# Moving a quarter of the product of dx and B from VectorE to GpSimd in a Mamba and mixture-of-experts block

## The chip, the cores and the metric

The kernel runs on one core of one Trainium2 chip. The time is the device time of that core in microseconds, from the first to the last instruction of one execution. Five engines take part: TensorE (PE in the rows), VectorE (DVE), ScalarE (ACT), GpSimd (POOL) and SyncE (SP, which issues the DMAs here). Each engine runs its own instructions in the order of the program and waits on semaphores for the others.

## The reference

The input is x of 8 x 1024 tokens x 256 channels, in float32. Two layers follow, each with a residual:

```python
x = x + layernorm(mamba(layernorm(x)))
x = x + layernorm(moe(layernorm(x)))
```

The part that matters is the state space recurrence in `mamba`, with 512 inner channels d and 16 states s:

```python
dA  = exp(dt[..., None] * A)                    # decay
dBx = dt[..., None] * Bm[:, :, None, :] * xc[..., None]
h   = dA_t * h + dBx_t                          # over 1024 tokens
y_t = einsum('bds,bs->bd', h, C_t)
```

`moe` routes each token to 4 of 16 experts, with a hidden width of 128 in each; all 16 experts are computed for all tokens and weighted.

## The kernel before

The 8192 tokens are cut into 16 chunks of 512 (CH), two per sequence. The program is a software pipeline over phases p from -2 to 17, and each phase has 16 groups, g = 0 to 15. In phase p the recurrence of chunk p runs, one group of (d, s) pairs after another. Beside it stand the projections, the convolution and dt of chunk p + 1, the output projection and the routing of chunk p - 1 and, 26 groups later than the recurrence, one expert per group.

A group G (counted over all phases, 256 in all) holds 128 partitions x 4 blocks x 512 tokens of the state in the tile hs: a partition is a pair of channel and state, and the 4 blocks (beta = 0 to 3, NBETA = 4) are different channels. hs has three buffers (NH). The tile dxr holds dt times xc for four groups (one channel tile M), replicated over the partitions by a DMA, in two buffers; Bb and Cb hold B and C, one slot for each of the four state sets s. A group goes through these steps:

- `inputs(G)`, VectorE, L858: hs = dxr * B for all four blocks at once, one instruction of 128x2048. It adds to the semaphore s_u.
- `decay`, ScalarE, L501: dA = exp(A dt), one block at a time, in two PSUM tiles.
- `scan(G, beta)`, VectorE, L872: h = dA h + hs in place, four instructions of 128x512. dA is read from PSUM. In the second chunk of a sequence it starts from `carry`.
- `read_out(G)`, GpSimd, L761: hs = hs * C, 128x2048. It adds to s_c.
- `add_states(G)`, TensorE, L446: the sum over states into the PSUM tile Y. It adds to s_y, and its buffer of hs is free.

An expert goes from TensorE (`gate` L416, `up` L424) over ScalarE (tanh, L507), VectorE (`expert_gate` L987, `expert_up` L992) and GpSimd (`weigh` L751) back to TensorE (`down` L434).

The order on each engine is written out by hand in loops over the groups. On VectorE, group G is: L987, scan 0, L992, scans 1 to 3, then whatever belongs to this g (L879 gates a finished Y; L831 convolution steps at g = 2 and 3; small statistics at g = 4, 6 and 12; L891 at 5; the routing L924 to L983 at 9; L847, which forms DX, at 10; L1003 at 13), and last `inputs(G + 1)`. GpSimd does per group: wait until s_u shows that `inputs(G)` is done, then `weigh`, then `read_out(G - 1)`. In chunks with an even number (phase without carry) the scans start from zero; in odd ones they read carry.

SP issues the loads of dxr (L227) and Bb (L235); before it overwrites a buffer it waits on s_u for the last product that reads it.

Of the kernel before, what the change touches and what calls it, by code (L numbers as in the profile page):

```python
# [70 lines left out]
def sandwich_kernel(nc, x, w_in, w_out, w_gu, w_dn, w_x, w_rt, cols, alog, ebias, consts, sel_dt, out):  # L71
    with ExitStack() as ctx:
# [7 lines left out]
        def sem(name):  # L80
            return ctx.enter_context(nc.semaphore(name))
# [53 lines left out]
        dxr = sb('dxr', [P, 2, NBETA, CH])  # L135
        Bb = sb('Bb', [P, NSIG, CH])
        Cb = sb('Cb', [P, NSIG, CH])
        hs = sb('hs', [P, NH, NBETA, CH])
# [25 lines left out]
        f_act = Steps(sem('f_act'), ['xT0', 'xT1', 'raw0', 'tap0', 'raw1', 'tap1', 'raw2', 'tap2', 'raw3', 'tap3', 'z0', 'silu_x', 'xd', 'dt', 'z1', 'z2', 'z3', 'silu_z'])  # L164
        f_dve = Steps(sem('f_dve'), [f'c{k}{m}' for m in DVE_CONV for k in range(HIST)] + ['hist', 'dx'])
        fp_full = sem('fp_full')
        s_u, s_dA, s_h, s_keep, s_c, s_y, y_gate = (sem(k) for k in ('s_u', 's_dA', 's_h', 's_keep', 's_c', 's_y', 'y_gate'))
        route = ['den', 'score', 'sfc', 'ps', 't1', 't2', 'gs', 'ggt', 'geq', 'gq', 'ga', 'gr', 'gm', 'tmp', 'top', 'gt', 'eq', 'ng', 'cs', 'cn', 'ok', 'sel', 'w', 'ws', 'we', 'wr', 'comb']
        p_dve = Steps(sem('p_dve'), ['w1', 'nb', 'x1', 'Bw1'] + rsqrt_names('q') + ['Bnb'] + route)
        p_act = Steps(sem('p_act'), ['xn0', 'xn1', 'rev0', 'rev1', 'nm', 'sq', 'ro', 'sum2', 'nm2', 'sq2', 'x2', 'x2T0', 'x2T1', 'sig', 'cmT'])  # L170
# [7 lines left out]
        ld_dx = [sem(f'ld_dx{k}') for k in range(4)]  # L178
        ld_B = [sem(f'ld_B{s}') for s in range(NSIG)]
# [22 lines left out]
        def _(sp):  # L202
# [18 lines left out]
            def load_dx(M, k):  # L221
                if M % MT == 0:
                    sp.wait_ge(st_dx, 16 * (M // MT + 1))
                if M >= 2:
                    sp.wait_ge(s_u, (M - 1) * NSIG)
                src = dx_d.rearrange('(M c k b) t -> M k c (b t)', k=2, b=2, c=CB)[M, k]
                sp.dma_start(dxr[:, M % 2, 2 * k:2 * k + 2, :].rearrange('p b t -> p (b t)'), src.unsqueeze(1).broadcast_to([CB, SG, 2 * CH])).then_inc(ld_dx[2 * (M % 2) + k], 16)  # L227

            def load_B(c, s):
                if s == 0:  # L230
                    sp.wait_ge(st_xd, 16 * (c + 1))
                if c > 0:
# [22 lines left out]
            for p, g, G in groups():  # L255
                c = p + 1
# [488 lines left out]
        @block.gpsimd  # L745
        def _(pool):

            def weigh(q):
                pool.wait_ge(m_w, q + 1)
                pool.wait_ge(ld_cm[q % 2], 16 * (q // 2 + 1))  # L750
                pool.tensor_tensor(th[:, q % NTH, :], th[:, q % NTH, :], cmb[:, q % 2, :], ALU.mult).then_inc(m_a, 1)  # L751

            def read_out(G):
                c, m, s = (G // GPC, G // NSIG % MT, G % NSIG)
                if m == 0:
                    pool.wait_ge(ld_C[s], 16 * (c + 1))
                if c % HALVES < HALVES - 1:
                    pool.wait_ge(s_keep, c // HALVES * GPC + G % GPC + 1)
                else:
                    pool.wait_ge(s_h, (G + 1) * NBETA)  # L760
                pool.tensor_tensor(hs[:, G % NH, :, :], hs[:, G % NH, :, :], Cb[:, s, :].unsqueeze(1).broadcast_to([P, NBETA, CH]), ALU.mult).then_inc(s_c, 1)  # L761
            for p, g, G in groups():
                if 0 <= G < NGRP:
                    pool.wait_ge(s_u, G + 1)
                q = expert_at(G - 2)
                if q is not None:
                    weigh(q)
                if 0 <= G - 1 < NGRP:
                    read_out(G - 1)

        @block.vector
        def _(dve):
# [76 lines left out]
            def inputs(G):  # L849
                c, M, s = (G // GPC, G // NSIG, G % NSIG)  # L850
                if s == 0:
                    for k in range(2):
                        dve.wait_ge(ld_dx[2 * (M % 2) + k], 16 * (M // 2 + 1))
                if M % MT == 0:
                    dve.wait_ge(ld_B[s], 16 * (c + 1))
                if G >= NH:
                    dve.wait_ge(s_y, G - NH + 1)
                dve.tensor_tensor(hs[:, G % NH, :, :], dxr[:, M % 2, :, :], Bb[:, s, :].unsqueeze(1).broadcast_to([P, NBETA, CH]), ALU.mult).then_inc(s_u, 1)  # L858

            def scan(G, beta):  # L860
# [227 lines left out]
```

## Time and profile before

| what | value |
|---|---|
| median of the timed runs | 2791.8 us (3 runs, 2788.87 to 2792.28) |
| span of the profiled execution | 2792.0 us |
| TensorE, VectorE, GpSimd busy | 86%, 88%, 53% |
| L858, product of dx and B | 256 x 2.292 us = 586.6 us on VectorE |
| L761 and L751 | 256 x 4.528 us and 256 x 1.271 us on GpSimd |
| mean granted clock of TensorE | 0.953 |

The profile is of one execution, recorded by the hardware. A row of the timeline gives the start, the duration, the engine, the line of the kernel, what it writes and reads, the shape and the count of instructions merged into it. The idle time before it and what ended that stand in brackets. A window row gives the busy time of each engine in one stretch, with the count of its instructions, then TensorE's granted clock and the DMA share. Busy shares over the whole span mix stretches with different limits, so the rows below are taken from one phase (chunk 8, groups 128 to 143).

### The profile page before, as it was taken

Reading aid. Unit: us, or ns where it says so; the run is one execution under the profiler, and the core shown is the slowest. Engines: PE = TensorE matmul, PEld = TensorE weight load, DVE = VectorE, ACT = ScalarE, POOL = GpSimd, SP = SyncE. Lnnn points to the kernel's source line nnn. Section 1 sums busy time; section 2 is a strip of 40 time slices with the busy share of each in tenths; the row PEclk is TensorE's granted clock in tenths of the full one; section 3 lists DMA queues with packets and bytes.
Section 4 is the critical chain, followed back from the end, with each engine's and each line's share of the span. In section 5 each row is a group of like instructions: output and inputs, shape, how many; then the busy total and the mean of one; then the engine's idle time right before and its main releaser. Section 6 shows DMA issues by size and latency. Waiting matters only on the chain.

```text
span 2792.0 us, 27042 instructions
## 1 busy us (share of the span) xinstructions
PE 2414.2 (86%) x8416; PEld 1179.1 (42%) x8416; DVE 2455.6 (88%) x3265; ACT 1628.2 (58%) x3312; POOL 1474.8 (53%) x516
## 2 busy tenths in 40 slices
PE   4556799898989989899998989899898989988898
PEld 1112254443534444354444435354444445444454
DVE  1799998989899998989989898999989899899642
ACT  3566565666666566665666656665666665654331
POOL 0355564646556564655555465565646556565511
PEclk9677899999999999999999999999999999999999
DMA  1532332425244252524435252433525233352221
GB/s 36 226 107 90 129 139 96 160 94 177 77 144 140 98 170 81 188 74 143 133 105 172 79 184 83 136 130 105 179 79 175 95 124 128 100 177 70 64 76 59
DMA packets 164811, 336.65 MB, mean 121 GB/s; under 512 B 15771, under 2 KB 73404, under 8 KB 156220
## 3 DMA queue, kind: packets, MB, share of 16 engines
q1 hardware_dynamic: 164668, 334.93, 35.8%
q8 instruction: 67, 1.10, 0.2%
q14 instruction: 76, 0.62, 0.1%
HBM read 291.35 MB, written 43.52 MB: 120 GB/s over the span
## 4 chain that ended last, share of the span: by engine, by line
PE 42%; DVE 39%; issue 10%; ACT 9%; DMA 0%; SPq 0%; DVEq 0%; ACTq 0%
DVE hs L872 17%; DVE hs L858 9%; PE Gp L416 8%; PE Up L424 7%; PE MY L434 7%; PE FP L343 5%; PE FP L353 4%; PE FP L379 3%; PE Y L446 3%; DVE th L987 3%; DVE th L992 3%; PE FP L361 1%; ACT XC L571 1%; ACT XB L519 1%; ACT DX L636 1%
## 5 line engine op out<-in xcount | busy, mean ns | idle before, releaser
L761 POOL TENSOR_TENSOR hs<-hs,Cb 128x2048 f32<-128x2048 f32 x256 | 1159.1, 4528 | 203.7 <-DVE hs L858 203.7
L501 ACT ACTIVATE dA<-dtr,A 128x512 f32<-128x512 f32 x1024 | 699.7, 689 | 771.3 <-DVE hs L872 768.7
L751 POOL TENSOR_TENSOR th<-th,cmb 128x512 f32<-128x512 f32 x256 | 325.4, 1271 | 1096.8 <-DVE hs L858 980.7
L872 DVE TENSOR_TENSOR_SCAN hs<-dA,carry,hs 128x512 f32<-128x512 f32 x512 | 627.2, 1264 | 31.7 <-ACT dA L501 31.4
L416 PE MATMUL Gp<-x2T,Wgu 128*128 128x512 f32 x1024 | 530.4, 642 | 129.2 <-DVE th L987 129.0
L872 DVE TENSOR_TENSOR_SCAN hs<-dA,hs 128x512 f32<-128x512 f32 x512 | 596.2, 1203 | 50.6 <-ACT dA L501 50.1
L858 DVE TENSOR_TENSOR hs<-dxr,Bb 128x2048 f32<-128x2048 f32 x256 | 586.6, 2292 | 13.4 <-DMA dxr<-dx_d 12.3
L434 PE MATMUL MY<-Wdn,th 128*128 128x256 f32 x2048 | 486.3, 380 | 0.0
L424 PE MATMUL Up<-x2T,Wgu 128*128 128x512 f32 x1024 | 486.2, 597 | 0.0
L434 PEld LDWEIGHTS MY<-Wdn,th 128*128 128x128 f32 x2048 | 383.6, 190 | 136.5 <-issue 84.6
L416 PEld LDWEIGHTS Gp<-x2T,Wgu 128*128 128x128 f32 x1024 | 183.6, 198 | 473.4 <-issue 259.1
L446 PE MATMUL Y<-hs,Cst 128*32 128x512 f32 x2048 | 291.0, 642 | 21.5 <-POOL hs L761 21.5
L343 PE MATMUL FP<-xT,Win 128*128 128x512 f32 x512 | 262.1, 636 | 49.6 <-ACT SZ L565 15.8
L424 PEld LDWEIGHTS Up<-x2T,Wgu 128*128 128x128 f32 x1024 | 190.7, 192 | 260.8 <-issue 208.4
L987 DVE SCALAR_TENSOR_TENSOR th<-th,Gp 128x512 f32<-128x512 f32 x256 | 173.5, 678 | 68.1 <-ACT th L507 68.1
L507 ACT ACTIVATE th<-Gp 128x512 f32<-128x512 f32 x256 | 149.0, 582 | 114.8 <-PE Gp L416 114.8
L992 DVE TENSOR_TENSOR th<-Up,th 128x512 f32<-128x512 f32 x256 | 170.0, 664 | 10.0 <-PE Up L424 9.3
L343 PEld LDWEIGHTS FP<-xT,Win 128*128 128x128 f32 x512 | 95.8, 199 | 193.9 <-issue 94.5
L353 PE MATMUL FP<-XB,Kdiag 128*128 128x512 f32 x256 | 121.6, 620 | 11.6 <-ACT XB L551 11.6
L379 PE MATMUL FP<-Wout,SZ 128*128 128x256 f32 x512 | 122.6, 383 | 3.1 <-ACT DX L611 3.1
L379 PEld LDWEIGHTS FP<-Wout,SZ 128*128 128x128 f32 x512 | 98.0, 192 | 31.2 <-issue 14.3
L446 PEld LDWEIGHTS Y<-hs,Cst 128*32 128x32 f32 x2048 | 41.2, 110 | 149.5 <-issue 109.0
(131 smaller groups left out, 1827.1 us busy)
## 6 DMA issues: line engine op xcount, KB each, us to landing
dtr<-dt_d SPq DMA_DIRECT2D x64, 1024.0 KB, 5.5
dxr<-dx_d SPq DMA_DIRECT2D x128, 512.0 KB, 7.2
cmb<-cm_d SPq DMA_DIRECT2D x256, 256.0 KB, 3.6
Wdn<-in_w_dn SPq DMA_DIRECT2D x256, 128.0 KB, 3.5
dt_d<-XB SPq DMA_DIRECT2D x16, 1024.0 KB, 4.3
dx_d<-DX SPq DMA_DIRECT2D x16, 1024.0 KB, 5.8
Bb<-bc_d SPq DMA_DIRECT2D x64, 256.0 KB, 3.1
Cb<-bc_d SPq DMA_DIRECT2D x64, 256.0 KB, 4.0
```

What stands on the lines that cost most here:

```text
L343: mm = pe.matmul(FP[:, :], Win[:, q, c0:c0 + P], xT[:, q, :], start=q == 0, stop=q == KM - 1)
L379: pe.matmul(o, SZ[:, c % 2, m, b * P:(b + 1) * P], Wout[:, m, :], start=m == 0, stop=False)
L416: mm = pe.matmul(Gp[:, :], Wgu[:, k, e, 0:DE], x2T[:, c % 2, k, :], start=k == 0, stop=k == KM - 1)
L424: mm = pe.matmul(Up[:, :], Wgu[:, k, e, DE:2 * DE], x2T[:, c % 2, k, :], start=k == 0, stop=k == KM - 1)
L434: mm = pe.matmul(MY[b // 2][:, (b % 2) * DM:(b % 2 + 1) * DM], th[:, q % NTH, b * P:(b + 1) * P], Wdn[:, q % NWD, :], start=e == 0 and b % ...
L446: mm = pe.matmul(Y[beta * CB:(beta + 1) * CB, :], sel_y, hs[:, G % NH, beta, :], start=False, stop=s == NSIG - 1, tile_position=(0, beta * ...
L501: act.activation(dA[h % 2][:, :], dtr[:, M % 2, beta, :], ACT.Exp, scale=A[:, k:k + 1]).then_inc(s_dA, 1)
L751: pool.tensor_tensor(th[:, q % NTH, :], th[:, q % NTH, :], cmb[:, q % 2, :], ALU.mult).then_inc(m_a, 1)
L761: pool.tensor_tensor(hs[:, G % NH, :, :], hs[:, G % NH, :, :], Cb[:, s, :].unsqueeze(1).broadcast_to([P, NBETA, CH]), ALU.mult).then_inc(s ...
L858: dve.tensor_tensor(hs[:, G % NH, :, :], dxr[:, M % 2, :, :], Bb[:, s, :].unsqueeze(1).broadcast_to([P, NBETA, CH]), ALU.mult).then_inc(s_ ...
L872: dve.tensor_tensor_scan(hv, dA[h % 2][:, :], hv, first, ALU.mult, ALU.add).then_inc(s_h, 1)
L987: dve.scalar_tensor_tensor(out=th[:, q % NTH, :], in0=th[:, q % NTH, :], scalar=1.0, in1=Gp[:, :], op0=ALU.add, op1=ALU.mult).then_inc(m_v, 1)
```

## The change

The product of dx and B is split. VectorE forms it for the blocks 0 to 2 of a group (128x1536), and GpSimd forms it for block 3 (128x512) in the new `last_input(G + 1)`, at the end of its group G, behind `read_out(G - 1)`. It waits for the same loads and the same free buffer (s_y) as VectorE's part, and adds to a new semaphore s_u3. The scan of block 3 waits for s_u3, and so do SP's loads into dxr and Bb. GpSimd's wait at the top of its group is on s_u alone, as before.

```diff
@@ SP: load_dx, load_B
                     sp.wait_ge(s_u, (M - 1) * NSIG)
+                    sp.wait_ge(s_u3, (M - 1) * NSIG)
...
                     sp.wait_ge(s_u, c * GPC - NSIG + s + 1)
+                    sp.wait_ge(s_u3, c * GPC - NSIG + s + 1)
@@ GpSimd
+            def last_input(G):
+                c, M, s = (G // GPC, G // NSIG, G % NSIG)
+                if s == 0:
+                    pool.wait_ge(ld_dx[2 * (M % 2) + 1], 16 * (M // 2 + 1))
+                if M % MT == 0:
+                    pool.wait_ge(ld_B[s], 16 * (c + 1))
+                if G >= NH:
+                    pool.wait_ge(s_y, G - NH + 1)
+                pool.tensor_tensor(hs[:, G % NH, NBETA - 1, :], dxr[:, M % 2, NBETA - 1, :], Bb[:, s, :], ALU.mult).then_inc(s_u3, 1)
...
                 if 0 <= G - 1 < NGRP:
                     read_out(G - 1)
+                if 0 <= G + 1 < NGRP:
+                    last_input(G + 1)
@@ VectorE: inputs, scan
-                dve.tensor_tensor(hs[:, G % NH, :, :], dxr[:, M % 2, :, :], Bb[:, s, :].unsqueeze(1).broadcast_to([P, NBETA, CH]), ALU.mult).then_inc(s_u, 1)
+                dve.tensor_tensor(hs[:, G % NH, 0:NBETA - 1, :], dxr[:, M % 2, 0:NBETA - 1, :], Bb[:, s, :].unsqueeze(1).broadcast_to([P, NBETA - 1, CH]), ALU.mult).then_inc(s_u, 1)
...
+                if beta == NBETA - 1:
+                    dve.wait_ge(s_u3, G + 1)
                 dve.wait_ge(s_dA, h + 1)
```

GpSimd's order before, in a phase with experts; th is the expert's activation, hs the state:

```order
L761 TENSOR_TENSOR hs<-hs,Cb 128x2048 [waits s_h,ld_C0]
L751 TENSOR_TENSOR th<-th,cmb 128x512 [waits ld_cm0,m_w,s_u]
L761 TENSOR_TENSOR hs<-hs,Cb 128x2048 [waits s_h,ld_C1]
L751 TENSOR_TENSOR th<-th,cmb 128x512 [waits ld_cm1,m_w,s_u]
L761 TENSOR_TENSOR hs<-hs,Cb 128x2048 [waits s_h,ld_C2]
```

GpSimd's order now; L753 is the old L751, L773 the old L761, L763 the new product:

```order
L753 TENSOR_TENSOR th<-th,cmb 128x512 [waits ld_cm1,m_w,s_u]
L773 TENSOR_TENSOR hs<-hs,Cb 128x2048 [waits s_h]
L763 TENSOR_TENSOR hs<-dxr,Bb 128x512 [waits s_y]
L753 TENSOR_TENSOR th<-th,cmb 128x512 [waits ld_cm0,m_w,s_u]
L773 TENSOR_TENSOR hs<-hs,Cb 128x2048 [waits s_h]
L763 TENSOR_TENSOR hs<-dxr,Bb 128x512 [waits s_y]
```

The product stands behind the read-out of the group before and ahead of the wait on s_u that opens the next group.

VectorE's order before, at the end of group 9 and in group 10 of a phase with carry:

```order
L983 SCALAR_TENSOR_TENSOR comb<-DX 128x64 [waits p_dve,fp_full]
L879 TENSOR_TENSOR SZ<-Y,SZ 128x512 [waits s_y]
L858 TENSOR_TENSOR hs<-dxr,Bb 128x2048 [waits s_y]
L987 SCALAR_TENSOR_TENSOR th<-th,Gp 128x512 [waits m_th]
L872 SCALAR_TENSOR_TENSOR hs<-dA,carry,hs 128x512 [waits s_dA,s_keep,s_u]
L992 TENSOR_TENSOR th<-Up,th 128x512 [waits m_v,m_u]
L872 SCALAR_TENSOR_TENSOR hs<-dA,carry,hs 128x512 [waits s_dA] x3
L847 TENSOR_TENSOR DX<-XB,XC 128x2048 [waits p_dve,f_act]
```

The same place now; L872 is the shortened product, L888 the scan, L1003 and L1008 the old L987 and L992, L861 the old L847:

```order
L999 SCALAR_TENSOR_TENSOR comb<-DX 128x64 [waits p_dve,fp_full]
L895 TENSOR_TENSOR SZ<-Y,SZ 128x512 [waits s_y]
L872 TENSOR_TENSOR hs<-dxr,Bb 128x1536 [waits s_y]
L1003 SCALAR_TENSOR_TENSOR th<-th,Gp 128x512 [waits m_th]
L888 SCALAR_TENSOR_TENSOR hs<-dA,carry,hs 128x512 [waits s_dA,s_keep,s_u]
L1008 TENSOR_TENSOR th<-Up,th 128x512 [waits m_v,m_u]
L888 SCALAR_TENSOR_TENSOR hs<-dA,carry,hs 128x512 [waits s_dA] x2
L888 SCALAR_TENSOR_TENSOR hs<-dA,carry,hs 128x512 [waits s_dA,s_u3]
L861 TENSOR_TENSOR DX<-XB,XC 128x2048 [waits p_dve,f_act]
```

Nothing changes its place on VectorE; the product is shorter, and the last scan has a wait more.

## Rows read from the trace of the kernel before

**Rows 1.** The page: span, then busy us (share of the span) and instructions of each engine.
```profile
span 2792.0 us, 27042 instructions
...
PE 2414.2 (86%) x8416; PEld 1179.1 (42%) x8416; DVE 2455.6 (88%) x3265; ACT 1628.2 (58%) x3312; POOL 1474.8 (53%) x516
```

**Rows 2.** The page, costliest groups: count | busy us, mean ns | idle before, releaser.
```profile
L761 POOL TENSOR_TENSOR hs<-hs,Cb 128x2048 f32<-128x2048 f32 x256 | 1159.1, 4528 | 203.7 <-DVE hs L858 203.7
...
L751 POOL TENSOR_TENSOR th<-th,cmb 128x512 f32<-128x512 f32 x256 | 325.4, 1271 | 1096.8 <-DVE hs L858 980.7
...
L858 DVE TENSOR_TENSOR hs<-dxr,Bb 128x2048 f32<-128x2048 f32 x256 | 586.6, 2292 | 13.4 <-DMA dxr<-dx_d 12.3
```

**Rows 3.** Windows, cut at ends of L858: groups 0, 1-6, 7-8, 9, 10 to 14; last phase.
```profile
core 0: us, PE busy (x) PEld busy (x) DVE busy (x) ACT busy (x) POOL busy (x), PEclk, DMA share, GB/s
1336.65:1344.63 7.98, 6.29 (x24) 3.69 (x24) 7.98 (x9) 4.34 (x9) 5.75 (x2) 1.00 0.99 344
1344.63:1407.05 62.42, 62.42 (x219) 32.40 (x217) 58.80 (x83) 39.59 (x104) 34.56 (x12) 1.00 0.26 83
1407.05:1427.66 20.61, 17.05 (x61) 7.81 (x60) 15.98 (x17) 14.62 (x22) 11.54 (x4) 0.92 0.41 141
1427.66:1443.37 15.71, 15.50 (x66) 7.50 (x63) 14.55 (x40) 9.32 (x14) 5.74 (x2) 1.00 0.14 41
1443.37:1453.55 10.18, 8.49 (x32) 4.06 (x32) 10.18 (x9) 3.85 (x7) 5.76 (x2) 1.00 0.24 88
1453.55:1461.53 7.98, 7.27 (x23) 3.49 (x20) 7.98 (x8) 4.35 (x8) 5.75 (x2) 1.00 0.64 232
1461.53:1472.72 11.19, 9.53 (x39) 4.09 (x37) 10.01 (x21) 9.41 (x28) 5.77 (x2) 1.00 0.20 59
1472.72:1482.30 9.58, 7.55 (x26) 3.33 (x26) 9.58 (x10) 5.93 (x8) 5.75 (x2) 1.00 0.79 281
1482.30:1490.27 7.97, 6.42 (x24) 3.03 (x24) 7.97 (x8) 6.26 (x11) 5.75 (x2) 1.00 0.64 190
...
2487.91:2496.00 8.09, 7.45 (x26) 4.95 (x27) 8.09 (x8) 3.28 (x5) 5.76 (x2) 1.00 0.14 49
```

**Rows 4.** Timeline, a bare period without carry: start us, us, engine, line [idle before].
```profile
1482.38 1.27 POOL L751 TENSOR_TENSOR th<-th,cmb 128x512 f32<-128x512 f32 x1 [3.84 <-DVE hs L858]
...
1483.60 4.52 POOL L761 TENSOR_TENSOR hs<-hs,Cb 128x2048 f32<-128x2048 f32 x1
...
1484.53 3.44 DVE L872 TENSOR_TENSOR_SCAN hs<-dA,hs 128x512 f32<-128x512 f32 x3
...
1487.89 2.38 DVE L858 TENSOR_TENSOR hs<-dxr,Bb 128x2048 f32<-128x2048 f32 x1
```

**Rows 5.** Timeline, a bare period with carry.
```profile
1329.86 4.52 POOL L761 TENSOR_TENSOR hs<-hs,Cb 128x2048 f32<-128x2048 f32 x1
...
1334.39 2.26 DVE L858 TENSOR_TENSOR hs<-dxr,Bb 128x2048 f32<-128x2048 f32 x1
```

**Rows 6.** Timeline, after the last scans: GpSimd at work as L891 is issued.
```profile
2657.18 1.26 POOL L751 TENSOR_TENSOR th<-th,cmb 128x512 f32<-128x512 f32 x1 [9.59 <-DVE th L992]
...
2657.85 1.68 DVE L891 TENSOR_TENSOR x<-DX,x 128x1024 f32<-128x1024 f32 x1 [0.75 <-ACT DX L629]
```

**Rows 7.** Timeline, VectorE, group 13: L1003, GpSimd idle.
```profile
1478.88 1.21 DVE L1003 TENSOR_TENSOR x<-my,x 128x1024 f32<-128x1024 f32 x1
```

**Rows 8.** Timeline, group 9.
```profile
1433.36 1.07 PE L446 MATMUL Y<-hs,Cst 128*32 128x512 f32 x8
...
1434.55 0.23 DVE L928 TENSOR_TENSOR DX<-DX,Ebias 128x64 f32<-128x64 f32 x1
```

**Rows 9.** Timeline, VectorE, group 12.
```profile
1467.96 0.17 DVE L801 TENSOR_SCALAR z_w<-z_s 128x4 f32<-128x4 f32 x1 [0.77 <-ACT XB L519]
```

**Rows 10.** Timeline, group 3: VectorE frees Gp, TensorE fills it again.
```profile
1363.16 0.68 DVE L987 SCALAR_TENSOR_TENSOR th<-th,Gp 128x512 f32<-128x512 f32 x1
...
1367.31 1.98 PE L416 MATMUL Gp<-x2T,Wgu 128*128 128x512 f32 x4
```

More of the change, by code:

```diff
@@ L166, in sandwich_kernel @@
         fp_full = sem('fp_full')
-        s_u, s_dA, s_h, s_keep, s_c, s_y, y_gate = (sem(k) for k in ('s_u', 's_dA', 's_h', 's_keep', 's_c', 's_y', 'y_gate'))
+        s_u, s_u3, s_dA, s_h, s_keep, s_c, s_y, y_gate = (sem(k) for k in ('s_u', 's_u3', 's_dA', 's_h', 's_keep', 's_c', 's_y', 'y_gate'))
         route = ['den', 'score', 'sfc', 'ps', 't1', 't2', 'gs', 'ggt', 'geq', 'gq', 'ga', 'gr', 'gm', 'tmp', 'top', 'gt', 'eq', 'ng', 'cs', 'cn', 'ok', 'sel', 'w', 'ws', 'we', 'wr', 'comb']
```

## The prediction, made before the changed kernel ran

> **What bounds the kernel now.** I read the page's busy times first [rows 1]: TensorE 86% and VectorE 88% of a span of 2792.0 us, GpSimd 53%. No engine is full over the whole span, so the question is which is full where. The costliest groups come next [rows 2]: the product of dx and B on VectorE takes 2.292 us 256 times, and GpSimd has two jobs per group, 4.528 us (h times C) and 1.271 us (weighting an expert). Then I cut one phase (16 groups) into periods, each from the end of one L858 to the end of the next [rows 3]. Four kinds of stretch appear:
> - Groups 1 to 6, 62.42 us: TensorE is busy all of it. VectorE has 3.6 us of idle time.
> - Groups 7 and 8, 20.61 us: a chain over ScalarE and TensorE up to the routing sigmoid. VectorE idles 4.6 us.
> - Groups 9 to 15, 1427.66 to 1498.25: VectorE is busy 68.3 of 70.6 us (group 15 reads like 14; 10, 11, 13, 14 and 15 have no gap). It sets the end there.
> - Group 0: VectorE is full, and TensorE's long stretch starts from its last scan.
> So only time on VectorE in groups 9 to 15 counts directly: 7 periods per phase. I call a period bare when VectorE does only L987, four scans, L992 and L858: 7.97 us without carry (even phases), 8.1 us with it (odd phases; the last window of rows 3 is one).
>
> **The sizes.** A product of 128x2048 takes 2.26 us undisturbed [rows 5], a two-input one of 128x1024 takes 1.21 us [rows 7]; the line between them gives 1.21 + (2.26 - 1.21)/2 = 1.74 us for 128x1536. VectorE saves 0.53 us per group (0.48 to 0.57 if the fixed part is off). The same shape on GpSimd, all operands in SBUF, is L751: 1.27 us [rows 2]. Its work per period becomes 1.27 + 4.53 + 1.27 = 7.05 us. The new wait of scan 3 on s_u3 costs nothing: the product is ready at the latest 1.3 us into the next period, and scan 3 starts some 4.3 us into it [rows 4].
>
> **What GpSimd and VectorE do to each other.** This decides the sign. VectorE's L891 is issued 0.67 us into GpSimd's L751 and takes 1.68 us [rows 6]; its twin in shape takes 1.21 us alone [rows 7]. The overlap is 2657.18 + 1.26 - 2657.85 = 0.59 us, the extra is 0.47 us: L891 did nothing until 0.12 us before GpSimd's end. Sharing at half speed would have given only 0.30 us. The product L858 shows it too: in rows 4 it starts 0.23 us before L761's end and takes 2.38 instead of 2.26 us, 0.12 us more. Scans, L987 and L992, which take one input from PSUM, run inside L761 at their usual time (3.44 us for three) [rows 4]. So a VectorE operation with two SBUF inputs waits for a GpSimd operation in progress. Today the wait on s_u at the top of GpSimd's loop starts its two jobs just after L858, and L761 ends 5.82 us into the period (1483.60 + 4.52 - 1482.30), while L858 is ready at 5.59 us without carry (1487.89 - 1482.30) and at 5.84 with it (L761 begins 1.30 us into a period, so that of rows 5 began at 1328.56, and L858 starts at 1334.39): they just miss each other. The new product takes exactly the place behind L761, 5.78 to 7.05 us, where L858 stands.
>
> No row shows the opposite case, GpSimd arriving while VectorE holds. The Trainium skill (SBUF — State Buffer, "SBUF: two separate sides") says that whichever of the two starts first has the shared pair for its whole instruction and the other is fully blocked; by that the sum is the one below, 2831 us, and without the blocking of GpSimd it is that of rival B.
>
> **Sum, even phase** (times within the period; the change against today):
> - Bare, GpSimd on time: L858 has waited since 5.59, goes at 5.70, ends 7.44: -0.53. The product follows at 7.4 and reaches 1.25 us into the next period.
> - Bare, GpSimd 1.25 late: L761 ends at 6.95, L858 runs 6.83 to 8.57, the product after it again: +0.59.
> - Group 9: a routing chain of 27 small operations follows the sigmoid, which it already waits for, so what groups 7 and 8 save is absorbed. GpSimd's product needs s_y, raised by TensorE's L446, which ends 1434.43; then it runs for 1.27 us just as L928 (two SBUF inputs) is due at 1434.55 [rows 8]. L928 waits about 1.05 us: +1.05 - 0.53 = +0.52.
> - Group 10: L847 (2.3 us, two SBUF inputs) takes the place at 5.70 to 7.96, the waiting product 7.9 to 9.2, L858 9.1 to 10.83 against 10.18: +0.65.
> - Group 11, bare: -0.53.
> - Group 12: L801, due at 6.43 [rows 9], is held to 6.83, the product enters between two small operations and holds the chain until 8.05; 2.26 us of it are left, then 1.74: 12.05 against 11.19: +0.86.
> - Group 13: L1003, due at 6.16 [rows 7], waits to 6.93: +0.77 - 0.53 = +0.24.
> - Groups 14 and 15, bare: -0.53 and +0.59.
> Sum +1.80 us.
>
> **Odd phase**: the scans are longer, L858 is due at 5.84, after the product has started; every bare period waits to 6.93 and ends at 8.67: +0.57, with no backlog. Group 9 +0.52, group 10 +0.56, 11 +0.57, 12 -0.16, 13 -0.02, 14 and 15 +0.57 each. Sum +2.61 us.
>
> Mean 2.2 us, times 14 phase changes, is 31 us. The last phase has no next front to feed and 8 bare periods of 8.1 us, of which the last of [rows 3] is one: 8 x 0.57 = 5 us. The first phases run without L751 and partly wait for a slow start; I take 3 us (0 to 8). Total +39 us on 2792.0 us: 2831 us. The median of the timed runs, 2791.8 us, lies 0.2 us from the profiled span, so nothing is added.
>
> **What stays hidden.** In groups 0 to 3 VectorE falls behind by 0.6 + 0.1 + 1.7 + 0.7 = 3.1 us, because the three L831 of groups 2 and 3 (two SBUF inputs) meet the product too. TensorE has 1367.31 - 1363.84 = 3.5 us between L987 and the gate matmul that waits for it [rows 10], and VectorE catches up in its idle time of groups 4 and 6. I cost this at nothing; without the cover it is 1 to 3 us per phase. SP's loads of dxr and B now wait for s_u3 as well, up to 1.25 us later; they are issued two or more periods ahead: nothing.
>
> **Rivals.**
> A. The cover of groups 1 to 6 fails (TensorE waits for L987 or for ScalarE's evacuations behind late scans): +1 to +3 us in 14 phases, 2845 to 2870 us. For it: 3.1 of 3.5 us of slack are used. Against: the delays come stepwise, and VectorE idles in 4.
> B. GpSimd is never held by VectorE: it keeps its schedule, no backlog. Even bare periods all give -0.53, group 10 -0.53, group 12 -0.04: the even sum is -1.4, the odd stays; mean +0.6, 14 x 0.6 + 5 + 3 = 16: 2808 us. Nothing in the trace excludes it.
> C. The other side: the two do not hinder each other, or the product mostly falls into gaps. Then VectorE's 0.53 us counts in groups 9 to 15 in full: 14 x 7 x 0.53 = 52, and some 15 periods at both ends 8: 2732 us. GpSimd's 7.05 us would fit under 7.44. It decides from the point where the wait on GpSimd is under 0.53 us per period; rows 4 and 6 speak against it.
> D. Small operations pay nothing (only whole L858, L847 and L1003 are held): group 9 -0.53, group 12 -0.15; sums -0.3 and +1.6, mean +0.65, total 2809 us, or with luck in 0 to 3 no change at all.
> E. The change does not do what it says, for instance because scan 3 waits for s_u3 and the time moves there: same as A in size.
>
> **How the numbers follow.** Forecast 0.60 with its own range 2818 to 2845; A (with E) 0.16; B and D together 0.15, of which a third ends within 0.2% (5.6 us, what a measurement can tell from no change); C and smaller gains 0.09. The range of 2802 to 2868 us takes in B, D and most of A. Slower 0.60 + 0.16 + 0.10 = 0.86, same 0.05, faster 0.09.
>
> **What would show it.** L858's successor with 1.74 us alone, but a mean well above that (about 2.3 to 2.7 us with the waits), its overlap with GpSimd ending 0.12 us before GpSimd does. Bare periods of 7.44 and 8.57 in turn in even phases, 8.67 in odd ones. GpSimd's busy share from 53% to about 65%. Group 9 longer by 0.5 us, with one small operation of about 1.2 us. Groups 1 to 6 unchanged at 62.4 us. It is wrong if L858's successor starts and ends at 1.74 us while GpSimd's product is running, or if bare periods fall below 7.6 us in odd phases.

## The result: 0.8% slower, 22 us of the 39 forecast

| | before | after |
|---|---|---|
| median of 4 runs each, us | 2792.04 (2788.87 to 2794.82) | 2813.85 (2812.87 to 2814.76) |
| ratio, 95% interval | | 1.0079 (1.0065 to 1.0093) |
| span of the profiled execution, us | 2792.0 | 2811.9 |

The forecast was 2831 us with a range of 2802 to 2868. The direction holds, and so does the mutual blocking of the two engines; the size was forecast 1.8 times too large. Half of the miss lies in the phases with carry (odd), where a step of the forecast failed. The time lies in the range all the same.

In the changed kernel the lines of the program have moved: L753 is the old L751 (weighting an expert), L763 GpSimd's new product, L773 the old L761 (h times C), L872 VectorE's product (old L858), L888 the scans (old L872), L944 and L946 the old L928 and L930 of the routing. First its page: the busy times and four of the costliest groups, in the columns of [rows 1] and [rows 2].

```profile
span 2811.9 us, 27803 instructions
...
PE 2421.8 (86%) x8416; PEld 1181.7 (42%) x8416; DVE 2493.3 (89%) x3265; ACT 1627.8 (58%) x3312; POOL 1986.5 (71%) x772
...
L773 POOL TENSOR_TENSOR hs<-hs,Cb 128x2048 f32<-128x2048 f32 x256 | 1158.2, 4524 | 60.0 <-DVE hs L872 60.0
...
L763 POOL TENSOR_TENSOR hs<-dxr,Bb 128x512 f32<-128x512 f32 x256 | 527.5, 2060 | 100.8 <-DMA dxr<-dx_d 83.5
L872 DVE TENSOR_TENSOR hs<-dxr,Bb 128x1536 f32<-128x1536 f32 x256 | 506.5, 1978 | 12.2 <-DMA dxr<-dx_d 12.1
...
L845 DVE SCALAR_TENSOR_TENSOR XC<-XB,Cols,XC 128x512 f32<-128x512 f32 x96 | 112.5, 1172 | 14.3 <-ACT XC L557 12.0
```

VectorE has a quarter less of the product to form and yet is busy 38 us longer than in [rows 1]. That is what blocking looks like here: not as idle time but as long instructions. The product means 1.978 us where 1.76 is its undisturbed mean (an experiment below), L763 2.060 us where the same shape takes 1.27 in L753, and L845, which nobody touched, went from 753 ns (L831) to 1172.

Next the windows of the changed kernel, cut as [rows 3]: two bare periods of an odd phase, then an even phase with its groups 0, 1 to 6, 7 and 8, 9, 10, 11, 12, 13, 14 and 15.

```profile
core 0: us, PE busy (x) PEld busy (x) DVE busy (x) ACT busy (x) POOL busy (x), PEclk, DMA share, GB/s
1325.21:1332.77 7.56, 6.48 (x24) 3.03 (x24) 7.56 (x8) 5.55 (x9) 7.49 (x3) 1.00 0.54 193
1332.77:1341.22 8.45, 6.55 (x24) 3.03 (x24) 8.45 (x8) 4.83 (x9) 8.45 (x4) 1.00 0.53 176
1341.22:1349.67 8.45, 6.78 (x28) 3.85 (x32) 8.45 (x8) 4.83 (x9) 8.45 (x4) 1.00 0.93 326
1349.67:1412.84 63.17, 62.72 (x220) 32.74 (x213) 60.77 (x83) 39.59 (x104) 45.41 (x19) 1.00 0.26 83
1412.84:1431.62 18.78, 15.22 (x55) 7.01 (x54) 14.89 (x16) 14.12 (x22) 14.37 (x6) 0.91 0.46 154
1431.62:1448.81 17.19, 16.07 (x68) 7.83 (x66) 14.99 (x40) 9.24 (x14) 8.18 (x4) 1.00 0.15 48
1448.81:1459.53 10.72, 9.32 (x40) 4.06 (x32) 10.72 (x9) 3.85 (x7) 9.03 (x3) 1.00 0.23 80
1459.53:1466.97 7.44, 6.41 (x17) 3.00 (x18) 7.44 (x8) 4.29 (x8) 7.36 (x3) 1.00 0.70 233
1466.97:1478.91 11.94, 10.07 (x41) 4.58 (x39) 10.77 (x21) 9.02 (x29) 8.08 (x4) 1.00 0.20 56
1478.91:1488.72 9.81, 8.98 (x26) 4.08 (x26) 9.81 (x10) 6.59 (x9) 6.97 (x3) 0.83 0.79 281
1488.72:1496.17 7.45, 6.42 (x24) 3.04 (x24) 7.45 (x8) 5.53 (x10) 7.38 (x3) 1.00 0.63 194
1496.17:1504.61 8.44, 6.49 (x24) 3.03 (x24) 8.44 (x8) 4.90 (x10) 8.44 (x4) 1.00 0.58 177
```

The first bare period behind a gap of GpSimd takes 7.44 to 7.56 us and each further one 8.44 or 8.45, group 0's among them; in those GpSimd has no idle time at all (8.45 of 8.45). The even phase from group 0 to 15 is 163.39 us; the same windows before add up to 161.59 [rows 3, with group 15 as long as 14]: +1.80. In groups 1 to 9 the cuts shift against one another because L872 isn't on the path there; take only their sum. GpSimd's 71% on the page is not work alone: by its undisturbed means it has 7.07 us of work per group, the rest is waiting inside its rows.

The timeline of the changed kernel shows how a short and a long period arise (start us, us, engine, line). Even phase, GpSimd:

```profile
1490.02 4.53 POOL L773 TENSOR_TENSOR hs<-hs,Cb 128x2048 f32<-128x2048 f32 x1
1494.51 2.78 POOL L763 TENSOR_TENSOR hs<-dxr,Bb 128x512 f32<-128x512 f32 x1
1497.25 1.26 POOL L753 TENSOR_TENSOR th<-th,cmb 128x512 f32<-128x512 f32 x1
1498.48 4.52 POOL L773 TENSOR_TENSOR hs<-hs,Cb 128x2048 f32<-128x2048 f32 x1
```

and VectorE's products of the two periods:

```profile
1494.31 1.85 DVE L872 TENSOR_TENSOR hs<-dxr,Bb 128x1536 f32<-128x1536 f32 x1
...
1501.76 2.85 DVE L872 TENSOR_TENSOR hs<-dxr,Bb 128x1536 f32<-128x1536 f32 x1
```

L872 is issued 0.24 us before L773 ends (1490.02 + 4.53 = 1494.55), waits 0.1 us and runs to 1496.16. GpSimd's product, listed from 1494.51, takes 2.78 us instead of 1.27: it stood still until L872 was through and ends 1.13 us after it. So L753 starts 1.08 us into the period, where L751 started at 0.08 [rows 4], L773 ends at 1503.00, and the next L872, ready at 1501.76, takes 2.85 us. From there it repeats: in the run of bare periods at the start of the last phase of the recurrence GpSimd's read-out comes every 8.45 us. In the same columns:

```profile
2488.85 4.52 POOL L773 TENSOR_TENSOR hs<-hs,Cb 128x2048 f32<-128x2048 f32 x1
2493.32 2.79 POOL L763 TENSOR_TENSOR hs<-dxr,Bb 128x512 f32<-128x512 f32 x1
...
2497.31 4.52 POOL L773 TENSOR_TENSOR hs<-hs,Cb 128x2048 f32<-128x2048 f32 x1
...
2505.76 4.51 POOL L773 TENSOR_TENSOR hs<-hs,Cb 128x2048 f32<-128x2048 f32 x1
```

Start to start: 1.23 us from L753 to L773, 4.47 to L763, 2.76 with the wait to the next L753. That is a loop in which L753, L773, L872 and L763 follow one another and none beside another, 8.45 us in all, where VectorE alone would need 7.44 (5.70 and 1.74). GpSimd *is* held by VectorE. The Trainium skill (SBUF — State Buffer, "SBUF: two separate sides") says so: whichever starts first holds the pair of SBUF ports that the two share for its whole instruction. By that rule, the trace agrees: 2.78 us against 1.27.

Group 9 in the changed kernel, one row of TensorE, one of GpSimd, two of VectorE:

```profile
1438.40 1.07 PE L448 MATMUL Y<-hs,Cst 128*32 128x512 f32 x8
...
1439.58 1.35 POOL L763 TENSOR_TENSOR hs<-dxr,Bb 128x512 f32<-128x512 f32 x1 [1.13 <-PE Y L448]
...
1439.58 0.23 DVE L944 TENSOR_TENSOR DX<-DX,Ebias 128x64 f32<-128x64 f32 x1
1439.84 1.14 DVE L946 TENSOR_TENSOR DX<-DX 128x32 f32<-128x32 f32 x1
```

The wait that was forecast is there, on the next small operation: L946 takes 1.14 us; the next operation of its shape, L947, takes 0.18, and before it was 0.19 for L930.

The rest I read phase by phase, by two stretches: front, from the last scan of group 0 to the end of the routing sigmoid, and back, from there to the last scan of the next group 0. Ends of rows, us:

| | front even | front odd | back even | back odd |
|---|---|---|---|---|
| before | 91.37 | 91.15 | 70.47 | 71.32 |
| after | 91.85 | 91.98 | 71.80 | 71.72 |
| change | +0.48 | +0.83 | +1.33 | +0.40 |

These are phases 4 to 8. Of those behind them all but one read otherwise in the changed kernel: front 90.2 or 93.2 us, back up to 72.7, which over two phases adds up to within 0.7 us of the same (see the last section). The mean of the two kinds is (1.81 + 1.23) / 2 = 1.52 us. The whole difference of the spans, 19.8 us, I cut at the last scan of group 0 of a phase. Up to that of phase 1 the changed kernel is 3.2 us ahead (219.00 against 222.20). The 14 phase changes from there to phase 15 give +18.6 (14 x 1.52 would be 21; phase 1 alone gives -0.7), and what is behind gives +4.4: 2.0 in the groups of phase 15 and 2.4 after its last scan.

### The profile page after: what moved, and what is told of

It is laid out like the page before. It is cut to its first block, busy times and chain, and to the rows that moved or that the text cites. A ratio compares the mean times of both kernels' runs of the same rounds, so it can differ in the third digit from the quotient of the medians.

```text
span 2811.9 us, 27803 instructions
## 1 busy us (share of the span) xinstructions
PE 2421.8 (86%) x8416; PEld 1181.7 (42%) x8416; DVE 2493.3 (89%) x3265; ACT 1627.8 (58%) x3312; POOL 1986.5 (71%) x772
## 4 chain that ended last, share of the span: by engine, by line
PE 40%; DVE 39%; issue 11%; ACT 9%; POOL 0%; DMA 0%; DVEq 0%; SPq 0%; ACTq 0%; POOLq 0%
DVE hs L888 16%; DVE hs L872 8%; PE Gp L418 7%; PE MY L436 6%; PE Up L426 6%; PE FP L345 6%; PE FP L355 4%; PE FP L381 3%; DVE th L1008 3%; DVE th L1003 3%; PE Y L448 3%; PE FP L363 1%; ACT XC L573 1%; ACT XB L521 1%; ACT dA L503 1%
## 5 line engine op out<-in xcount | busy, mean ns | idle before, releaser
L773 POOL TENSOR_TENSOR hs<-hs,Cb 128x2048 f32<-128x2048 f32 x256 | 1158.2, 4524 | 60.0 <-DVE hs L872 60.0
L753 POOL TENSOR_TENSOR th<-th,cmb 128x512 f32<-128x512 f32 x256 | 324.7, 1269 | 647.8 <-DVE hs L872 530.3
L888 DVE TENSOR_TENSOR_SCAN hs<-dA,carry,hs 128x512 f32<-128x512 f32 x512 | 626.6, 1262 | 28.4 <-ACT dA L503 28.0
L418 PE MATMUL Gp<-x2T,Wgu 128*128 128x512 f32 x1024 | 542.8, 655 | 111.8 <-DVE th L1003 111.8
L888 DVE TENSOR_TENSOR_SCAN hs<-dA,hs 128x512 f32<-128x512 f32 x512 | 595.7, 1202 | 43.5 <-ACT dA L503 42.8
L763 POOL TENSOR_TENSOR hs<-dxr,Bb 128x512 f32<-128x512 f32 x256 | 527.5, 2060 | 100.8 <-DMA dxr<-dx_d 83.5
L872 DVE TENSOR_TENSOR hs<-dxr,Bb 128x1536 f32<-128x1536 f32 x256 | 506.5, 1978 | 12.2 <-DMA dxr<-dx_d 12.1
L1003 DVE SCALAR_TENSOR_TENSOR th<-th,Gp 128x512 f32<-128x512 f32 x256 | 173.3, 677 | 71.2 <-ACT th L509 71.2
L1008 DVE TENSOR_TENSOR th<-Up,th 128x512 f32<-128x512 f32 x256 | 169.8, 663 | 9.3 <-PE Up L426 8.7
L845 DVE SCALAR_TENSOR_TENSOR XC<-XB,Cols,XC 128x512 f32<-128x512 f32 x96 | 112.5, 1172 | 14.3 <-ACT XC L557 12.0
```

The costliest lines, as they stand in the source:

```text
L418: mm = pe.matmul(Gp[:, :], Wgu[:, k, e, 0:DE], x2T[:, c % 2, k, :], start=k == 0, stop=k == KM - 1)
L763: pool.tensor_tensor(hs[:, G % NH, NBETA - 1, :], dxr[:, M % 2, NBETA - 1, :], Bb[:, s, :], ALU.mult).then_inc(s_u3, 1)
L872: dve.tensor_tensor(hs[:, G % NH, 0:NBETA - 1, :], dxr[:, M % 2, 0:NBETA - 1, :], Bb[:, s, :].unsqueeze(1).broadcast_to([P, NBETA - 1, CH] ...
L1003: dve.scalar_tensor_tensor(out=th[:, q % NTH, :], in0=th[:, q % NTH, :], scalar=1.0, in1=Gp[:, :], op0=ALU.add, op1=ALU.mult).then_inc(m_v, 1)
```

## The experiments

Ratios are against the kernel before on the same chip. Where a short condition stands for an edit, the waits on s_u3 are counted to match.

**1. VectorE's saving alone.**
```
-                if 0 <= G + 1 < NGRP:
-                    last_input(G + 1)
+            dve.memset(hs[:, :, NBETA - 1, :], 0.0)     # once, at the start
...
-                if beta == NBETA - 1:
-                    dve.wait_ge(s_u3, G + 1)
```


> The saving alone: VectorE forms the product for the blocks 0 to 2, and nobody forms it for block 3 (its state stays zero, so its part of y is missing from the result). No GpSimd operation and no s_u3 is added. Theory L (the two engines exclude each other, and VectorE's time counts in groups 9 to 15 and in the product at the end of group 0): 8 x 0.53 us per phase and some 20 periods at both ends, 2792 - 14 x 4.2 - 10 = about 2723 us; bare periods 7.44 us (even) and 7.56 us (odd). Rival W (the saving on VectorE is worth little, because ScalarE or TensorE is next in those groups): 2760 to 2790 us.


Measured 2730.1 us, 0.9782 (0.9767 to 0.9796). Its page:
```profile
span 2729.4 us, 27043 instructions
...
L869 DVE TENSOR_TENSOR hs<-dxr,Bb 128x1536 f32<-128x1536 f32 x256 | 450.5, 1760 | 13.5 <-DMA dxr<-dx_d 12.8
```
and its windows: a bare odd period, groups 1 to 6, a bare even period.
```profile
1288.47:1296.03 7.56, 6.48 (x24) 3.03 (x24) 7.56 (x8) 6.05 (x9) 5.75 (x2) 1.00 0.66 192
...
1311.04:1373.26 62.22, 62.12 (x219) 32.77 (x220) 55.76 (x83) 40.31 (x105) 34.60 (x12) 1.00 0.27 88
...
1447.48:1454.92 7.44, 6.42 (x24) 3.03 (x24) 7.44 (x8) 6.27 (x10) 5.75 (x2) 1.00 0.64 211
```
The 0.53 us counts in full where VectorE is full (7.97 to 7.44) and not in groups 1 to 6. The saving is worth 61 us, 7 less than expected: the even fronts of phases 4 to 14 are 0.8 to 0.9 us longer, at a mean granted clock of 0.963 instead of 0.981. So what GpSimd's product costs in the changed kernel is some 83.

**2. GpSimd's work alone.** VectorE keeps the whole product; GpSimd multiplies 128x448 into a spare tile.
```
+                if G > 0:
+                    pool.wait_ge(s_u3, G)
-                pool.tensor_tensor(hs[:, G % NH, NBETA - 1, :], dxr[:, M % 2, NBETA - 1, :], Bb[:, s, :], ALU.mult).then_inc(s_u3, 1)
+                pool.tensor_tensor(spare[:, :], dxr[:, M % 2, NBETA - 1, 0:CH - 64], Bb[:, s, 0:CH - 64], ALU.mult).then_inc(s_u3, 1)
```


> The cost alone: VectorE forms all four blocks as before, and GpSimd forms a product of 128x448 of the same inputs at the place of the change, into a spare tile that nobody reads (the result is the reference's). GpSimd's work is 1.27 + 4.53 + about 1.13 = 6.9 us per period, under the 7.97 us of a bare period, so by time alone it would fit. Theory L: the undelayed bare period stays at 7.97 or 8.10 us, the next one is 8.96 us, groups 10, 12 and 13 lose 0.4 to 1.2 us each, group 9 loses 0.8 us to one small operation; 4.9 to 5.7 us per phase: 2792 + 74 + 6 = about 2872 us. Rival N (no exclusion, the loss of the change comes from the new semaphore waits or the loads): 2792 to 2800 us.


Measured 2895.3 us, 1.0377 (1.036 to 1.0394). Two bare odd periods of it:
```profile
1363.91:1372.01 8.10, 7.06 (x32) 3.03 (x24) 8.10 (x8) 5.69 (x10) 8.03 (x3) 1.00 0.63 180
1372.01:1380.85 8.84, 6.55 (x24) 3.03 (x24) 8.84 (x8) 4.30 (x8) 8.84 (x4) 1.00 0.59 186
```
The same alternation with the whole product: 8.10 and 8.84. It cost 23 us more than expected. From phase 2 to 15 a phase costs 6.2 us where 4.9 to 5.7 were expected: +3.3 to +4.5 us in the back (one phase +5.9) and in most fronts +1.6 to +3.4; the rest of the miss lies in the first phases and behind phase 15. With a whole product behind each wait the cover of groups 0 to 6 leaks: TensorE is 0.75 to 0.9 us late from group 0 on, and 1.9 to 2.0 from the first fill of the convolution. Cost alone +105 and saving alone -61 make +44; together they were +22, so they are not additive. I read it so: with the whole product the time that both engines must share is longer by 0.5 us per group, and more of it lies above what VectorE fills anyway.

**3. The same jobs and waits, but GpSimd writes only.** Block 3 is zero in this run and the next.
```
-                pool.tensor_tensor(hs[:, G % NH, NBETA - 1, :], dxr[:, M % 2, NBETA - 1, :], Bb[:, s, :], ALU.mult).then_inc(s_u3, 1)
+                pool.memset(hs[:, G % NH, NBETA - 1, :], 0.0).then_inc(s_u3, 1)
```


> As the changed kernel, but GpSimd's instruction for block 3 is a memset of 128x512 to zero at the same place with the same waits and semaphore: it writes SBUF and reads nothing (block 3 is left out of the result). Theory L with reads alone (only a GpSimd operation that reads SBUF holds VectorE's two-input operations): as dve_only, about 2723 us, and VectorE's product at 1.74 us while the memset runs. Theory L with any access: VectorE waits for the memset too; for a memset of 0.3 to 1.3 us between 2740 and 2814 us. Rival S (the loss is in the waits on s_u3 and s_y and in GpSimd's queue, not in the reads): as the changed kernel, 2814 us.


Measured 2729.3 us, 0.978 (0.9766 to 0.9795). A bare odd period, GpSimd and then VectorE:
```profile
1287.42 4.51 POOL L773 TENSOR_TENSOR hs<-hs,Cb 128x2048 f32<-128x2048 f32 x1
1291.88 0.52 POOL L763 MEMSET hs<- 128x512 f32 x1
1291.94 1.73 DVE L872 TENSOR_TENSOR hs<-dxr,Bb 128x1536 f32<-128x1536 f32 x1
```
Every semaphore, every wait, and the write to hs are as in the changed kernel, and the time is that of experiment 1. Rival E (the time moves to scan 3's wait) is out; so is a cost of the waits of the loads as such. The memset is shorter than the product, so s_u3 comes earlier than in the changed kernel; there the profile itself settles it, since none of its waits of VectorE is put down to GpSimd: its scans sit idle for 72 us in all, 71 of them for ScalarE's dA. The memset runs beside VectorE's product and neither is longer for it.

**4. Two memsets**, 128x448 and 128x512, some 1.0 us together, nearer to the product's 1.27.
```
+                pool.memset(spare[:, :], 0.0)
+                pool.memset(hs[:, G % NH, NBETA - 1, :], 0.0).then_inc(s_u3, 1)
```


> As gp_memset, with two memsets at the place of the product, one of 128x448 into a spare tile and then the one of 128x512 (block 3 is left out of the result): together about 1.0 us, near the product's 1.27 us. If only reads on GpSimd hold VectorE, the length does not matter: 2725 to 2735 us, as dve_only. If any access held it and the first memset was only too short to meet VectorE's product, bare odd periods (product due at 5.84 us, memsets 5.8 to 6.8 us) would wait some 0.9 us: 2760 us or more.


Measured 2728.7 us, 0.9769 (0.9756 to 0.9782): GpSimd's time as such, up to this 1.0 us, costs nothing. What costs is an operation that reads SBUF (no run separates its reading from its arithmetic). That is the second half of the rule of the Trainium skill named above ("only against a GpSimd op that reads SBUF"), and by experiments 3 and 4 the trace agrees.

**5. The product ahead of the read-out** in GpSimd's loop.
```
+                if 0 <= G + 1 < NGRP:
+                    last_input(G + 1)
                 if 0 <= G - 1 < NGRP:
                     read_out(G - 1)
-                if 0 <= G + 1 < NGRP:
-                    last_input(G + 1)
```


> The changed kernel with the product moved on GpSimd from behind the read-out to ahead of it, so that it lies under the scans, which take one input from PSUM. Theory L: the total that must not overlap stays the same, only the read-out ends 1.27 us later, so every bare period waits until 6.95 us and lasts 8.7 us; in group 9 the product must wait for s_y until 7.9 us, and then the read-out of 4.5 us falls on the routing chain, some 4 us more. 6 to 9 us per phase more than before the change: 2880 to 2920 us. Rival P (what hurts is only that the product stands right behind the read-out, in VectorE's way): faster than the changed kernel, 2770 to 2805 us.


Measured 2978.9 us, 1.0677 (1.0661 to 1.0693): the right direction, 60 us above the upper end. Windows: a bare odd period, groups 1 to 6, group 9.
```profile
1418.72:1427.39 8.67, 6.55 (x24) 3.03 (x24) 8.67 (x9) 6.65 (x11) 6.97 (x3) 1.00 0.51 172
1444.73:1514.05 69.32, 65.44 (x232) 33.40 (x224) 68.35 (x83) 43.62 (x107) 42.05 (x18) 1.00 0.23 76
1531.42:1549.70 18.28, 12.51 (x52) 6.84 (x50) 17.45 (x40) 9.18 (x14) 7.01 (x3) 0.86 0.24 83
```
The bare period is as expected. Groups 1 to 6 take 69.3 us where 62.42 stood [rows 3], but groups 7 and 8 give half of that back (17.37 against 20.61); with group 9, at 18.28 against 15.71, the nine groups are 6.2 us longer. By last scans of group 0 a phase costs 10.95 us (from phase 2 to 15) where 6 to 9 were expected, and 34 us more were lost before, up to phase 2 (402.57 against 368.44), where none had been put down; those I have not traced. In group 9, on VectorE:
```profile
1537.21 0.55 DVE L942 RECIPROCAL DX<-DX 128x64 f32<-128x64 f32 x1
1537.80 3.85 DVE L944 TENSOR_TENSOR DX<-DX,Ebias 128x64 f32<-128x64 f32 x1
```
L773 runs from 1537.05 for 4.51 us. The reciprocal (one input) passes inside it in 0.55 us; L944, an operation of 0.23 us, is held until 1541.65, 0.09 us behind the end of L773. Rival D (small operations pay nothing) is out.

**6 and 7. Where is it lost?** The split is made only in groups 1 to 7 of each phase, or only in 8 to 15 and 0.
```
+def split(G):
+    return (G - 1) % GPC in (1, 2, 3, 4, 5, 6, 7)      # or in (8, ..., 15, 0)
...
+                if 0 <= G + 1 < NGRP and split(G + 1):
...
+                nb = NBETA - 1 if split(G) else NBETA
```


> The change only for the products formed at the end of groups 1 to 7 of each phase (7 of 16); the others stay whole on VectorE. Theory L with the places: groups 1 to 6 are bound by TensorE and 7 by ScalarE and TensorE, so neither VectorE's 0.53 us nor its waits count: 2788 to 2797 us. Rival U (the loss is spread evenly over the groups): 7/16 of 22 us, 2801 us. Rival A (the cover of groups 1 to 6 leaks): above 2805 us.

> The change only for the products formed at the end of groups 8 to 15 and 0 (9 of 16). Theory L with the places: the whole loss of the change is made here, 2809 to 2818 us. Rival U: 9/16 of 22 us, 2804 us.


Measured 2793.2 us, 0.9998 (0.9989 to 1.0007), and 2813.4 us, 1.0073 (1.006 to 1.0086). Within these intervals all of the loss is made in groups 8 to 0, where VectorE sets the end, and the cover of groups 1 to 6 holds against rival A's 1 to 3 us per phase. In the first of the two runs the convolution step means 1.053 us where it was 0.753: 96 times 0.3 are 29 us of blocked VectorE that cost nothing (40 us in the changed kernel, by L845).

**8. Split in odd phases only.**
```
+def split(G):
+    return (G - 1) // GPC % 2 == 1
```


> The change only in the phases with an odd number (with carry), whole products in the even ones. The prediction on record had the odd phases lose more (2.61 us each) than the even ones (1.80): then 2792 + 7 x 2.6 + 5, about 2815 us. By the trace of the changed kernel, in which VectorE's product slips in ahead of GpSimd's in every other bare odd period (7.56 and 8.46 us in turn instead of 8.67 each), the odd phases lose about 1.2 us each: 2800 to 2805 us.


Measured 2811.0 us, 1.0064 (1.005 to 1.0077): a miss. The odd back stretch is +0.43 (all but the first) and the even one +0.01, as expected. But the seam costs: group 0 of an even phase, whole product, behind a split group. Its window, and GpSimd's and VectorE's rows in it:
```profile
1341.33:1350.32 8.99, 7.31 (x32) 3.84 (x32) 8.99 (x8) 4.84 (x9) 6.83 (x3) 1.00 0.86 313
```
```profile
1343.64 4.52 POOL L784 TENSOR_TENSOR hs<-hs,Cb 128x2048 f32<-128x2048 f32 x1
...
1346.92 3.40 DVE L884 TENSOR_TENSOR hs<-dxr,Bb 128x2048 f32<-128x2048 f32 x1
```
GpSimd is still late from the split group before, and a product of 2.26 us takes 3.40 (window 8.99 us against 7.98 in [rows 3]). Most even fronts are 1.0 us longer at the same mean clock. Three of the six odd ones are 1.9 to 2.0 longer, but there TensorE's granted clock is lower as well (mean 0.963 against 0.981, see the last section), so the seam's share of those is not known. This experiment does not price the odd phases by themselves; what it shows is that one group's backlog is charged to the next.

**9 and 10. The race that the forecast had lost.** Two memsets of one column ahead of VectorE's product in odd phases are to make it a shade later; experiment 10 does the same to the kernel before, to price the memsets.
```
+                if c_odd(G):
+                    dve.memset(tiny[:, 0:1], 0.0)
+                    dve.memset(tiny[:, 1:2], 0.0)
```


> The changed kernel with two tiny memsets (128x1 each, about 0.07 us) on VectorE ahead of its product, in the phases with an odd number alone, so that the product falls due some 0.14 us later there, at about 5.98 instead of 5.84 us. Theory R (a race: VectorE's product goes first in odd bare periods only because GpSimd's product, listed as started at 5.79 us, has not yet taken the path at 5.84): now GpSimd's product holds it first, bare odd periods last about 8.7 us each instead of 7.56 and 8.46 in turn, group 10 takes 10.9 instead of 9.76 us, some 2.3 us more per odd phase: about 2830 us. Rival V (VectorE comes first whenever both ask): only the memsets' own time, 0.14 us in 8 or 9 periods of 7 phases: 2822 us, and the turns of short and long periods stay.

> The kernel before with the same two memsets ahead of the product in odd phases: their own cost without a second GpSimd product. Both theories: 0.14 us in 8 or 9 periods of 7 phases, 2792 + 8 = 2800 us; bare odd periods of 8.24 us.


Measured 2829.2 us, 1.0135 (1.0122 to 1.0148), and 2799.9 us, 1.0027 (1.0017 to 1.0037). In the odd phases of 9, two windows of bare periods and the rows of the first, GpSimd and VectorE:
```profile
1327.70:1336.39 8.69, 6.48 (x24) 3.03 (x24) 8.69 (x11) 6.65 (x11) 6.99 (x3) 1.00 0.61 169
1336.39:1345.05 8.66, 8.01 (x24) 3.71 (x24) 8.66 (x10) 3.71 (x6) 6.97 (x3) 0.80 0.66 222
```
```profile
1333.49 1.28 POOL L768 TENSOR_TENSOR hs<-dxr,Bb 128x512 f32<-128x512 f32 x1
1333.56 2.83 DVE L880 TENSOR_TENSOR hs<-dxr,Bb 128x1536 f32<-128x1536 f32 x1
1333.57 0.06 DVE L878 MEMSET tiny<- 128x1 f32 x1
```
In the changed kernel the same place reads:
```profile
1331.00 2.90 POOL L763 TENSOR_TENSOR hs<-dxr,Bb 128x512 f32<-128x512 f32 x1
1331.05 1.73 DVE L872 TENSOR_TENSOR hs<-dxr,Bb 128x1536 f32<-128x1536 f32 x1
```
In the changed kernel VectorE goes first here and takes 1.73 us; with the memsets ahead it loses and takes 2.83. Over all odd phases of the changed kernel, 18 of its products are listed less than 0.1 us behind GpSimd's, and 16 of them win; in experiment 9 there are 30, and all lose. The listed starts do not tell the two apart: the 16 winners are listed 0.00 to 0.06 us behind, the changed kernel's two losers 0.01 and 0.05, the 30 losers 0.03 to 0.08. The memsets, which the program has ahead of the product, are even listed behind it. So the experiment shows that two tiny operations ahead of the product turn the race, and what the turn costs, but not what decides it.

With the race lost the bare odd periods are the forecast's 8.67, one after another, and the odd back stretch is 73.8 us, +2.5 on the kernel before. Term by term, groups 9 to 15 of odd phase 7 (last scan to last scan, group 9 from the sigmoid) are now +0.37, +0.54, +0.57, -0.15, 0.00, +0.59 and +0.57, where the forecast had +0.52, +0.56, +0.57, -0.16, -0.02, +0.57 and +0.57. The even ones stay at +1.35.

Experiment 10 came out at its expected 2800 us, but by luck. The memsets were to make a bare odd period 8.24 us; it is 8.14, and the odd back reads 71.3 to 71.6, at most 0.3 more. Most of the 5.8 us between the profiled spans are four fronts 1.2 to 1.6 us longer, all at a mean clock of 0.963 instead of 0.981. So the memsets themselves cost next to nothing, and +2.5 is the race's price to within 0.3 us.

## Right and wrong, step by step

- **VectorE saves 0.53 us per group**: right. 1.76 us against 1.74 estimated; 61 us in all by experiment 1.
- **A two-input operation of VectorE waits for GpSimd's**: right, down to small ones (experiments 2, 3, 5). **GpSimd waits for VectorE's**, which no row before had shown: right (2.78 us), rival B out.
- **The new wait of scan 3 costs nothing; SP's later loads cost nothing**: right (experiment 3).
- **Even phase, +1.80 us**: right in the sum, and in kind. From last scan to last scan the terms came out (forecast in brackets) as group 9 +0.42 (+0.52), 10 +0.54 (+0.65), 11 -0.54 (-0.53), 12 +0.77 (+0.86), 13 +0.21 (+0.24), 14 -0.53 (-0.53), 15 +0.47 (+0.59), which is 1.34, and group 0 +0.48 (none). Two small errors cancel, which is luck. The backlog was taken as 1.25 us; GpSimd's next job starts 1.08 us into the period (1497.25 - 1496.17). And "TensorE's long stretch starts from its last scan" failed as the reason to leave out group 0's product. It runs after that scan, late by the backlog, and pushes VectorE's group 1, ScalarE's evacuations of the transposed input and so TensorE's first fills; every later fill that TensorE does in the front is +0.48.
- **Odd phase, +2.61 us: the step that failed.** "L858 is due at 5.84, after the product has started; every bare period waits to 6.93 and ends at 8.67." GpSimd's product is listed first, but by 0.05 us only, and in most of these periods VectorE's still wins. So odd bare periods go like even ones, 7.56 and then 8.45: two sum to 16.01 where two of 8.09 stood, -0.2 instead of +1.14. Experiment 9 undoes just this win and gets the forecast's 8.67 and +2.5. The prediction had itself named this as a sign of being wrong: bare periods below 7.6 us in odd phases. The back stretch is +0.40 instead of +2.61. The odd front adds 0.83, which was put at nothing. Of it 0.36 is group 0's, like the 0.48 of the even phase; 0.23 comes at the first convolution fill, where TensorE now waits for ScalarE's copy XB, late behind VectorE; and 0.26 comes at TensorE's matmuls behind the idle time of groups 7 and 8, of which more fall into the stretch at half clock. Odd phases are then +1.23 instead of +2.61 us: 1.4 x 7 = 10 us of the miss of 19. The wait for XB, in phase 7:
```profile
1226.29 0.30 PEld L355 LDWEIGHTS FP<-XB,Kdiag 128*128 128x128 f32 x2 [0.36 <-ACT XB L553]
```
- **"7.44 and 8.57 in turn"**: half right. Short and long come as forecast where at most two bare periods stand in a row, but they don't alternate: once GpSimd is late it stays so, 8.45 each.
- **The first phases +3, the last +5**: the first are -3.2, 6 us of the miss, and I have only the difference of the ends of rows. The last reads +4.4, near the forecast by luck. Its sum was 8 bare periods at +0.57, and the failed step is in it too: the eight periods that took 8.1 us take 8.44 to 8.47 (four), 8.66 (one) and 7.56 (three), +0.4 together. The rest of the +4.4 lies in other groups and, 2.4 us of it, behind the last scan, where no reason is shown. The 2 to 3 us that are left of the miss are the phase changes that gave less than the 1.52 of phases 4 to 8, phase 1 above all.
- **Hidden in groups 0 to 3**: right in even phases, but for group 0's own product; in odd ones the 0.23 us above leak. Experiment 6 shows no loss beyond its interval, so rival A is out at its size of 1 to 3 us per phase.
- **The signs**: L872's mean is 1.98 us, not 2.3 to 2.7. Only 52 of its 256 instructions took over 2.3 us, because GpSimd, once late, is the one that waits (L763 took over 2 us 113 times).
- **Rival C** (no hindrance, 2732 us): out, but it was a good estimate of what experiments 1, 3 and 4 then gave when GpSimd read nothing.
- **GpSimd's busy share** is 71% and not 65%: its waits are in its rows as well.

No version that was run beats the kernel before while computing all of it. The sum that should have come first: before, GpSimd's 5.75 us and VectorE's product of 2.26 exclude each other, together 8.0 in a bare period of 7.97 that VectorE fills anyway. After, it is 7.07 + 1.74 = 8.8 less some overlap at the ends, measured 8.45 once GpSimd is late. The move takes 0.52 us from VectorE and puts 1.27 on the sum that both share, and in bare periods that sum became the bound.

## What to carry to other kernels

Before moving elementwise work from VectorE to GpSimd, add up per period what of both engines must not overlap: GpSimd's operations that read SBUF and VectorE's with two SBUF inputs. If that sum is near the period already, as here, don't expect the move to save anything, whatever GpSimd's idle share says (47% here). And where two engines arrive within 0.1 us of each other, forecast both orders and give each a chance: in these runs the listed starts did not tell who won.

## What the runs showed of the hardware

- Blocking between the two engines shows as duration: VectorE's busy time rose by 38 us with less work, and its idle time names no culprit. Compare means of untouched operations (L845: 753 to 1172 ns).
- A GpSimd memset of 128x512 (0.53 us) holds no two-input VectorE operation and is not held; a product of 128x448 is and does.
- Held were also small operations with one tensor input: L802 (old L788), of 128x4 int32, took 1.19 us in most phases where it had taken 0.17, the time of its neighbour in [rows 9]. A reciprocal of 128x64 and the scans were not.
- In the race of the two products, VectorE's won whenever it was listed ahead of GpSimd's (by 0.02 us at the least), and lost whenever it was listed 0.15 us or more behind. Between 0 and 0.1 us behind it won 16 of 18 in the changed kernel, 18 of 26 in experiment 8 and none of 30 in experiment 9.
- TensorE's granted clock falls to 0.5 (1.2 GHz, the lower of its two levels, instead of 2.4) for 3.4 us near the end of the front, after an idle time of 3.56 us in groups 7 and 8. In most phases of both kernels it falls there, and in many again in the back stretch. Where the timing has shifted it stays low for 6.8 us, or does not fall at all in the front: fronts of the changed kernel are 90.2 to 90.3 us with none of it, 91.9 to 92.0 with 3.4 us and 93.2 with 6.8. This is 1.3 to 1.7 us either way per phase, as large as the effect studied, and no reading of a single phase is safe from it.
